# Cross attention on one core: the vector engine's out-projection work moved behind the low halves of K and of the weights

## The chip, the cores and the metric

One core of a Trainium2 chip runs the whole program in one launch. The metric is the device time in microseconds; the median of three runs stands for a kernel. The engines run side by side and meet through semaphores: TensorE (PE, with its weight loads as PEld), VectorE (DVE), ScalarE (ACT), GpSimd (POOL) and the queue engine SyncE (SP).

## The reference

Three layers with residuals follow each other; the change sits in the first, a cross attention of 16 batches: 64 latent rows (x) each look at 512 context rows plus the latents themselves, 8 heads of 64, everything in fp32.

```
x = x + xattn(ctx, layernorm(x), mask)
x = x + attn(layernorm(x))
x = x + ffn(layernorm(x))        # weights and activations in blockwise FP4

# xattn
xn = LN(ctx) * g_x + b_x ;  ln = LN(latents) * g_l + b_l
q = ln @ w_q ;  k, v = split(concat(xn, ln) @ w_kv)
attn = softmax(q k^T * scale, masked)
out = LN((attn v) @ w_out) * g_o + b_o

# fp4_quant_dequant of a weight, in blocks of 16
scale = max|w| / 6 ;  wn = w / scale ;  q = nearest E2M1 value(wn) * scale
```

## The kernel before

An fp32 product is computed as three matmuls on a high part (rounded to fp32r) and a low part (what the rounding left): high by high, high by low, low by high. `mm3` (L142) issues them; in the profile they are the lines L146, L147 and L148. ACT copies a result out of PSUM and so rounds it to its high half. DVE subtracts the high half from the full value and gets the low half: `split_lo` (L786, its instruction at L788). A transpose on PE is L412.

The order of the work on every engine is written out by hand as one software pipeline. A loop over batches b = 0 to 16 contains eight slots each. In slots 0 to 3 PE projects the keys of batch b, 128 rows at a time (`project_k`), after weighing the values of batch b-1. In slots 4 to 7 it computes the scores, transposes the next batch's normalised context and projects values. The FP4 quantisation of the FFN weights is woven in: 34 jobs of 11 DVE steps, a transpose on PE and a split into `sb_w_hi` (ACT) and `sb_w_lo` (DVE), laid out by `weight_plan` (L101), at most four steps a slot.

PE writes into PSUM banks 4 to 7, taken in turn (`Ring`, L87). A bank that is to be written for the second time waits until the unit that used it has been drained, and a key tile is drained only by DVE's low half of K (`lo_of_k`, L809).

Batches are finished in pairs: two of them make one tile of 128 rows. For a tile, the out-projection's work is spread over two loop turns. In an even turn b: `out_split` (L849, slot 5), the matmul (slot 6), and `out_stats` (L854, slot 7). In the odd turn behind it: `out_scale` (L860, slot 0) normalises `sb_y_row` (L762) and multiplies it by g_o (L864). POOL adds b_o (`shift_y`, L1603, instruction L1605). `out_add` (L866, slot 1) adds the residual (L869) and takes the statistics of the sum (L749, L755, L757).

POOL's own order in slot 0 of an odd turn is: store the weight job's halves to DRAM (`spill_weight`, L1607, two DMAs that wait for `sb_w_lo`), then the addition of b_o, and, in slot 1, the power that turns the next batch's variances into reciprocal roots (`sb_b_rstd`, L1578), which waits for DVE's `sb_b_ve` (L757).

In the same slots DVE also normalises the context of batch b+1 (`normalise`, L813): two statistics in slot 0, two in slot 1 with the four L755 and the L757 of `finish_stats`, and the four normalisations (L762 on `sb_ctx`) in slots 2 and 3. PE's transposes in slot 4 need all four.

Of the kernel before, what the change touches and what calls it, by code (L numbers as in the profile page):

```python
# [44 lines left out]
TURN_STEP, SPLIT_STEP = QUANT_STEPS, QUANT_STEPS + 1  # L45
# [55 lines left out]
def weight_plan():  # L101

    plan, at = {}, [0, 0]

    def advance(key, count):
        plan[key] = []
        for _ in range(count):
            if at[0] == NJ:
                return
            job, step = at  # L110
            plan[key].append((job, step))
            at[:] = [job + 1, 0] if step == SPLIT_STEP else [job, step + 1]
            if step + 1 == TURN_STEP:
                plan[key].append((job, TURN_STEP))
                at[1] = SPLIT_STEP
                return

    for b in range(1, NB):
        for slot in range(8):
            if slot != 3 or b % 2:  # L120
                advance((b, slot), 4)
    assert at[0] == NJ
    return plan


WEIGHTS = weight_plan()
# [40 lines left out]
def perceiver(nc, a, out):  # L167
    ctx = ExitStack()
    with ctx:
# [569 lines left out]
        def vector_program(e):  # L739
# [8 lines left out]
            def small_stats(src, i, st):  # L748
                e.bn_stats(st[0][:, i, :], src).then_inc(dve_chain.up())  # L749

            def finish_stats(first, n, st):
                stats, mv, ve, rstd = st
                for i in range(first, first + n):
                    on.wait_ge(dve_chain.sem, dve_chain.value)
                    e.bn_aggr(mv[:, i, :], stats[:, i, :]).then_inc(dve_chain.up())  # L755
                on.wait_ge(dve_chain.sem, dve_chain.value)
                e.tensor_scalar(ve[:, first:first + n], mv[:, first:first + n, 1], EPS_LN, None, ALU.add).then_inc(rstds.up())  # L757
                return rstds.value
# [27 lines left out]
            def split_lo(full, hi, lo, hi_sem, hi_value, done):  # L786
                on.wait_ge(hi_sem, hi_value)
                e.tensor_tensor(lo, full, hi.bitcast(F32), ALU.subtract).then_inc(done)  # L788
# [20 lines left out]
            def lo_of_k(b, n):  # L809
                bank, nth = took["k", b, n]  # L810
                split_lo(psum[:, bank, :], k_hi[:, n, context_keys], k_lo[:, n, context_keys], k_hi_done, C * b + n + 1, drained[bank])

            def normalise(b):  # L813
                src = [ctx_in[b % 2][:, k, :] for k in range(CS)]
                on.wait_ge(ctx_landed[b % 2], 16 * (b // 2 + 1))
                on.wait_ge(z_normed, CS * b)
                for i in range(CS):
                    small_stats(src[i], i, small_b)
                    yield
                nth = finish_stats(0, CS, small_b)  # L820
                yield
                for i in range(CS):
                    normal(src[i], src[i], i, small_b, nth, z_normed)
                    yield
# [17 lines left out]
            def normalise_p(b, n):  # L842
                i, j, idx = b % 2, n % 2, C * b + n
                on.wait_ge(exped, idx + 1)
                e.reciprocal(row_inv[:, n:n + 1], row_sum[i][:, n:n + 1]).then_inc(row_inverted)
                on.wait_ge(row_inverted, idx + 1)
                e.tensor_scalar(probs[j][:, :], probs[j][:, :], row_inv[:, n:n + 1], None, ALU.mult).then_inc(p_normed)

            def out_split(t):  # L849
                on.wait_ge(tile_hi_done, t + 1)  # L850
                attn = x3[:, t, :].rearrange("p (c n) -> p c n", c=C)
                e.tensor_tensor(tile_lo[:, :, :], attn, tile_hi[:, :, :].bitcast(F32), ALU.subtract).then_inc(tile_lo_done)

            def out_stats(t):  # L854
                bank, nth = took["y", t]
                on.wait_ge(drained[bank], nth)
                small_stats(y_row[:, :], t, small_o)
                return finish_stats(t, 1, small_o)
# [77 lines left out]
            def lo_of_weight(job):  # L936
                width = JOBS[job][4]
                bank, nth = took["w", job]
                k = width // P
                ps = psum[:, bank, 0:width].rearrange("p (m n) -> p m n", n=P)  # L940
                split_lo(ps, w_hi[:, 0:k, :], w_lo[:, 0:k, :], wt_hi_done, job + 1, drained[bank])
# [156 lines left out]
            def lam_products():  # L1098
                on.wait_ge(row_consts_landed, 128)
                for k in range(2):  # L1100
                    e.tensor_tensor_reduce(lams[:, 2 * k, :], lams[:, 2 * k, :], lams[:, 2 * k + 1, :], 1.0, 0.0, ALU.mult, ALU.add,
                                           lam[:, k:k + 1]).then_inc(lam_dots)

            def lam_difference():
                on.wait_ge(lam_exped, 1)
                e.tensor_tensor(lam[:, 4:5], lam[:, 2:3], lam[:, 3:4], ALU.subtract).then_inc(dve_chain.up())
                on.wait_ge(dve_chain.sem, dve_chain.value)
                e.tensor_scalar(lam[:, 5:6], lam[:, 4:5], LAMBDA_INIT, None, ALU.add).then_inc(lam_ready)
                e.tensor_scalar(lnwb[:, :], lnwb[:, :], 1.0 - LAMBDA_INIT, None, ALU.mult).then_inc(lnw_ready)

            def zero_pack(i):
                for h, r in enumerate(HEAD_ROWS):
                    e.memset(q_pack[i][r, :, :, HEAD_ROWS[1 - h]].bitcast(U32), 0).then_inc(q_zeroed[i])
                e.memset(vl_pack[i][LQ:P, :], 0.0).then_inc(b_zeroed)
# [35 lines left out]
            for b in range(NB + 1):  # L1150
                cur, old, nxt = b < NB, b >= 1, b + 1 < NB
                t_new = (b - 2) // 2 if b % 2 == 0 and b >= 2 else None
                t_out = (b - 3) // 2 if b % 2 == 1 and b >= 3 else None
                norm = normalise(b + 1) if nxt else iter(())
                for slot in range(8):
                    if old and slot == 0:
                        normalise_p(b - 1, 3)
                    if cur and slot >= 5:
                        normalise_p(b, slot - 5)
                    if b == 0 and slot == 3:  # L1160
                        lam_products()
                        for i in range(QK_BUFFERS):
                            on.wait_ge(qk_spilled[i], 32 if i < C else 16)
                        on.wait_ge(last_keys_spilled, 16 * C)
                        for h in range(2):
                            on.wait_ge(vl_spilled[h], 64)
                        zero_pack(1)
                        for i in range(2):
                            e.memset(p_t[i][LQ:P, CS, :], 0.0).then_inc(p_zeroed)
                    if b == 2 and slot == 2:  # L1170
                        lam_difference()
                    if cur and slot == 2:
                        mask_row(b)
                    if cur and slot >= 4:
                        largest(b, slot - 4)
                    if nxt and slot >= 4:
                        lo_of_z(b + 1, slot - 4)
                    advance(norm, (2, 3, 2, 9)[slot] if slot < 4 else 0)
                    for job, step in WEIGHTS.get((b, slot), ()):
                        if step < QUANT_STEPS:  # L1180
                            next(weight_steps)
                    if t_new is not None:
                        if slot == 5:
                            out_split(t_new)
                        if slot == 7:
                            o_nth = out_stats(t_new)
                    if t_out is not None:
                        if slot == 0:
                            out_scale(t_out, o_nth)
                        if slot == 1:  # L1190
                            out_add(t_out)
                    if cur and slot < 4:
                        lo_of_k(b, slot)
                    for job, step in WEIGHTS.get((b, slot), ()):
                        if step == SPLIT_STEP:
                            lo_of_weight(job)
                    if not cur:
                        if slot == 0:
                            normal_y(0)
                        advance(steps, 1)  # L1200
# [669 lines left out]
```

## Time and profile before

| what | us |
|---|---|
| median of 3 runs (lowest, highest) | 1054.09 (1053.99, 1055.0) |
| the profiled execution's own time | 1053.52 |
| its span, from the first to the last instruction | 1051.7 |
| PE busy | 998.7 |
| DVE busy | 781.1 |
| ACT busy | 434.1 |
| POOL busy | 146.3 |

PE is busy for 95% of the span, DVE for 74%. The granted clock of PE was at its upper level but for short stretches, 0.990 in the mean. The loop over batches that the change touches takes the time from about 90 to 690 us of the span. Times in rows are microseconds from the start of the span. In a row of the timeline the first number is the start, the second the duration; consecutive instructions of one engine overlap a little in it, because an instruction's record begins while its predecessor drains. The chain of waits has the same instructions without that overlap, and "issue" in it is time for which the profile shows no reason.

### The profile page before, as it was taken

What the parts mean: (1) busy time and instruction counts of PE and PEld (TensorE: products, weight loads), DVE (VectorE), ACT (ScalarE), POOL (GpSimd) and SP (SyncE); (2) the same over time, 40 slices, a digit from 0 to 9 for tenths busy, and PEclk for the clock granted to TensorE, in tenths of its full rate; (3) what the DMA queues carried; (4) which work ended last, traced back from release to release, by engine and by line L of the source; (5) the groups of instructions that cost most, each with busy time, mean ns of one, the idle gap of its engine ahead of it and who ended that gap; (6) DMA issues with size and microseconds to landing.
All of it is one profiled execution on the core that took longest, in us unless ns stands there. A gap on an engine that the chain in (4) does not pass through costs nothing.

```text
span 1051.7 us, 16613 instructions
## 1 busy us (share of the span) xinstructions
PE 998.7 (95%) x6468; PEld 783.2 (74%) x6468; DVE 781.1 (74%) x1672; ACT 434.1 (41%) x811; POOL 146.3 (14%) x163
## 2 busy tenths in 40 slices
PE   5999999999999999999999999999999879999997
PEld 4887888788788787887887888645555558888885
DVE  6455687896987987987988864276477578998984
ACT  3534565466446445644653653222232222222211
POOL 1310011210210211202111110032132000000000
PEclk9999999999999999999999999999999889999999
DMA  7856242342442444244434323070000350000000
GB/s 242 242 160 195 75 128 65 108 126 63 128 129 74 105 118 120 65 120 121 108 83 106 111 81 110 20 271 1 2 2 16 145 206 25 10 11 11 11 11 20
DMA packets 72446, 98.50 MB, mean 94 GB/s; under 512 B 38320, under 2 KB 47152, under 8 KB 70064
## 3 DMA queue, kind: packets, MB, share of 16 engines
q1 hardware_dynamic: 65008, 72.80, 23.5%
q0 software_dynamic: 7360, 24.65, 7.4%
q8 instruction: 51, 0.84, 0.3%
q14 instruction: 27, 0.22, 0.1%
HBM read 67.54 MB, written 29.88 MB: 93 GB/s over the span
## 4 chain that ended last, share of the span: by engine, by line
PE 73%; DVE 17%; ACT 5%; issue 3%; DMA 1%; SPq 0%; POOL 0%; DVEq 0%; ACTq 0%
PE ps_banks L146 15%; PE ps_banks L148 15%; PE ps_banks L147 15%; PE ps_banks L531 10%; PE ps_banks L412 7%; PE ps_banks L508 2%; PE ps_banks L654 2%; PE ps_banks L653 2%; PE ps_banks L655 2%; DVE sb_b_stats L749 1%; PE ps_banks L429 1%; DVE sb_wq_big L915 1%; DVE sb_w_q L923 1%; DVE sb_ctx L762 1%; DVE sb_kT_lo L788 1%
## 5 line engine op out<-in xcount | busy, mean ns | idle before, releaser
L146 PE MATMUL ps_banks<-sb_zT_hi,sb_wkv_hi 128*128 128x512 f32 x256 | 105.9, 414 | 6.1 <-DVE sb_kT_lo L788 6.1
L146 PE MATMUL ps_banks<-sb_wkv_hi,sb_zT_hi 128*128 128x512 f32 x256 | 104.8, 409 | 0.0
L148 PE MATMUL ps_banks<-sb_wkv_hi,sb_zT_lo 128*128 128x512 f32 x256 | 100.4, 392 | 0.0
L148 PE MATMUL ps_banks<-sb_zT_hi,sb_wkv_lo 128*128 128x512 f32 x256 | 100.2, 391 | 0.0
L147 PE MATMUL ps_banks<-sb_zT_lo,sb_wkv_hi 128*128 128x512 f32 x256 | 100.0, 391 | 0.0
L147 PE MATMUL ps_banks<-sb_wkv_lo,sb_zT_hi 128*128 128x512 f32 x256 | 99.8, 390 | 0.0
L1252 ACT ACTIVATE sb_kT_hi<-ps_banks 128x512 fp32r<-128x512 f32 x64 | 38.1, 596 | 145.4 <-PE ps_banks L148 145.4
L146 PE MATMUL ps_banks<-sb_wgu,sb_z_hi 128*128 128x512 f32 (+1 forms) x192 | 74.3, 387 | 1.0 <-DVE sb_z_lo L788 1.0
L147 PE MATMUL ps_banks<-sb_wgu,sb_z_hi 128*128 128x512 f32 (+1 forms) x192 | 72.6, 378 | 0.0
L148 PE MATMUL ps_banks<-sb_wgu,sb_z_lo 128*128 128x512 f32 (+1 forms) x192 | 72.6, 378 | 0.0
L839 DVE CUSTOM_DVE_ANT_0 sb_probs<-ps_banks,sb_maskbias 128x576 f32<-128x576 f32 x64 | 48.1, 751 | 29.3 <-PE ps_banks L148 29.3
L788 DVE TENSOR_TENSOR sb_zT_lo<-sb_zfull,sb_zT_hi 128x512 fp32r<-128x512 f32 x64 | 44.2, 691 | 31.4 <-ACT sb_zT_hi L1296 31.4
L788 DVE TENSOR_TENSOR sb_kT_lo<-ps_banks,sb_kT_hi 128x512 fp32r<-128x512 f32 x64 | 43.7, 683 | 31.4 <-ACT sb_kT_hi L1252 30.9
L1292 ACT ACTIVATE sb_zfull<-ps_banks,sb_cols 128x512 f32<-128x512 f32 x64 | 49.8, 778 | 29.5 <-PE ps_banks L412 29.5
L146 PEld LDWEIGHTS ps_banks<-sb_zT_hi,sb_wkv_hi 128*128 128x128 f32 x256 | 48.1, 188 | 17.9 <-DVE sb_kT_lo L788 7.7
L1252 ACT ACTIVATE sb_probsT<-ps_banks 128x512 f32<-128x512 f32 (+1 forms) x128 | 47.8, 430 | 27.3 <-PE ps_banks L412 27.3
L148 PEld LDWEIGHTS ps_banks<-sb_wkv_hi,sb_zT_lo 128*128 128x128 f32 x256 | 48.0, 188 | 10.8
L148 PEld LDWEIGHTS ps_banks<-sb_zT_hi,sb_wkv_lo 128*128 128x128 f32 x256 | 48.0, 188 | 10.6
L1316 ACT ACTIVATE sb_probs<-sb_probs,sb_neg_max 128x576 f32<-128x576 f32 x64 | 49.7, 776 | 12.9 <-DVE sb_neg_max L839 12.3
L147 PEld LDWEIGHTS ps_banks<-sb_wkv_lo,sb_zT_hi 128*128 128x128 f32 x256 | 48.3, 189 | 8.4
L147 PEld LDWEIGHTS ps_banks<-sb_zT_lo,sb_wkv_hi 128*128 128x128 f32 x256 | 48.2, 188 | 8.2
L146 PEld LDWEIGHTS ps_banks<-sb_wkv_hi,sb_zT_hi 128*128 128x128 f32 x256 | 48.2, 188 | 8.1
(228 smaller groups left out, 2425.0 us busy)
## 6 DMA issues: line engine op xcount, KB each, us to landing
sb_ctx<-in_ctx SPq DMA_DIRECT2D x16, 1024.0 KB, 5.9
sb_wgu<-scratch_wgu SPq DMA_DIRECT2D x8, 1024.0 KB, 9.1
scratch_wgu<-sb_w_hi POOLq DMA_DIRECT2D x22, 256.0 KB, 3.2
scratch_wgu<-sb_w_lo POOLq DMA_DIRECT2D x22, 256.0 KB, 3.2
sb_wdn<-scratch_wdn SPq DMA_DIRECT2D x2, 2816.0 KB, 13.1
scratch_q<-sb_a_qk POOLq DMA_DIRECT2D x8, 512.0 KB, 6.2
sb_qpack<-scratch_q SPq DMA_DIRECT2D x32, 128.0 KB, 5.9
sb_wgu<-scratch_wgu SPq DMA_DIRECT2D x4, 768.0 KB, 13.8
```

The source lines that it names most:

```text
L146: e.matmul(o, wh, xh, start=i == 0, stop=False)
L147: e.matmul(o, wh, xl, start=False, stop=False)
L148: m = e.matmul(o, wl, xh, start=False, stop=i == n - 1)
L412: m = e.transpose(psum[:, bank, k * P:(k + 1) * P], s, ident[:, :])
L508: m = e.matmul(o_space(r, n), value, p_t[j][:, k, r], start=k == CS, stop=k == CS - 1)
L531: m = e.matmul(o, w[:, c, :], x[:, c, :], start=c == 0, stop=c == C - 1)
L653: e.matmul(psum[:, bank, :], h_hi[:, c, :], wdn[0][:, c, :], start=first, stop=False)
L788: e.tensor_tensor(lo, full, hi.bitcast(F32), ALU.subtract).then_inc(done)
L839: e.tensor_tensor_reduce(blocks(probs[j][:, :], WIDE // 2), s_space[j], blocks(mask_bias[:, keys(b)], WIDE // 2), -1.0, F32_MAX, ALU.add, ...
L1252: e.activation(dst, src, ACT.Identity).then_inc(done)
L1292: e.activation(z_full[j][:, :], psum[:, bank, :], ACT.Identity, bias=cols[:, 1, c:c + 1], scale=cols[:, 0, c:c + 1]).then_inc(act_chain.up())
L1316: e.activation(probs[j][:, :], probs[j][:, :], ACT.Exp, bias=neg_max[:, n:n + 1], scale=-1.0, accum_out=row_sum[b % 2][:, n:n + 1]).then_i ...
```

## The change

Inside a slot of DVE's loop, three calls trade places with two others. `out_scale`, `out_add` and `out_stats` now stand behind `lo_of_k` and `lo_of_weight`; `out_split` stays in front. Nothing is added or removed, and no other engine's program differs.

```
                     for job, step in WEIGHTS.get((b, slot), ()):
                         if step < QUANT_STEPS:
                             next(weight_steps)
-                    if t_new is not None:
-                        if slot == 5:
-                            out_split(t_new)
-                        if slot == 7:
-                            o_nth = out_stats(t_new)
+                    if t_new is not None and slot == 5:
+                        out_split(t_new)
+                    if cur and slot < 4:
+                        lo_of_k(b, slot)
+                    for job, step in WEIGHTS.get((b, slot), ()):
+                        if step == SPLIT_STEP:
+                            lo_of_weight(job)
+                    if t_new is not None and slot == 7:
+                        o_nth = out_stats(t_new)
                     if t_out is not None:
                         if slot == 0:
                             out_scale(t_out, o_nth)
                         if slot == 1:
                             out_add(t_out)
-                    if cur and slot < 4:
-                        lo_of_k(b, slot)
-                    for job, step in WEIGHTS.get((b, slot), ()):
-                        if step == SPLIT_STEP:
-                            lo_of_weight(job)
```

The first place is DVE in slot 0 of an odd turn (b = 3, 5, ..., 13; at 15 there is no weight). `sb_kT_lo` and `sb_w_lo` are the low halves of K and of the weight, `sb_y_row` the out-projection's row, `sb_b_stats` the next context's statistics.

```order
 L887 TENSOR_SCALAR sb_wq_scale<-sb_wq_amax 128x32
 L891 RECIPROCAL sb_wq_inv<-sb_wq_scale 128x32
+L788 TENSOR_TENSOR sb_kT_lo<-ps_banks,sb_kT_hi 128x512
+L788 TENSOR_TENSOR sb_w_lo<-ps_banks,sb_w_hi 128x512
 L762 TENSOR_SCALAR sb_y_row<-sb_y_row,sb_lo_mv,sb_lo_rstd 128x512
 L864 TENSOR_TENSOR sb_y_row<-sb_y_row,sb_g_o 128x512
-L788 TENSOR_TENSOR sb_kT_lo<-ps_banks,sb_kT_hi 128x512
-L788 TENSOR_TENSOR sb_w_lo<-ps_banks,sb_w_hi 128x512
 L749 BN_STATS sb_b_stats<-sb_ctx 128x6 x2
 L755 BN_AGGR sb_b_mv<-sb_b_stats 128x2 x4
```

Both low halves move ahead of the two instructions on `sb_y_row`; what stands before and behind the four is as it was.

The second place is DVE in slot 1 of the same turns. `sb_x` is the residual tile, `sb_ly_...` its statistics.

```order
 L904 TENSOR_SCALAR sb_wq_big<-sb_wq_mag 128x512
 L907 TENSOR_SCALAR sb_wq_mag<-sb_wq_mag 128x512
+L788 TENSOR_TENSOR sb_kT_lo<-ps_banks,sb_kT_hi 128x512
 L869 TENSOR_TENSOR sb_x<-sb_x,sb_y_row 128x512
 L749 BN_STATS sb_ly_stats<-sb_x 128x6
 L755 BN_AGGR sb_ly_mv<-sb_ly_stats 128x2
 L757 TENSOR_SCALAR sb_ly_ve<-sb_ly_mv 128x1
-L788 TENSOR_TENSOR sb_kT_lo<-ps_banks,sb_kT_hi 128x512
 L830 TENSOR_SCALAR sb_maskbias<-sb_mask 128x512
```

The low half of the second key tile moves ahead of the four instructions of `out_add`. In slot 7 of the even turns nothing changes places, since neither a key tile nor a weight's split falls into it.

## Rows read from the trace of the kernel before

**Rows 1.** The page: busy time of each engine, share of the span, instructions
```profile
PE 998.7 (95%) x6468; PEld 783.2 (74%) x6468; DVE 781.1 (74%) x1672; ACT 434.1 (41%) x811; POOL 146.3 (14%) x163
```

**Rows 2.** Who PE waited for, whole span: total us, times, longest
```profile
PE ps_banks L146 <- DVE sb_kT_lo L788: 6.1, 6, 1.1
...
PE ps_banks L412 <- DVE sb_w_q L923: 3.5, 5, 0.8
```

**Rows 3.** Timeline of PE in turn 3: start, us, [idle before <- releaser]
```profile
193.79 0.27 PE L494 MATMUL ps_banks<-sb_ident,sb_probs 128*64 128x128 f32 x1
195.16 0.50 PE L146 MATMUL ps_banks<-sb_zT_hi,sb_wkv_hi 128*128 128x512 f32 x1 [1.09 <-DVE sb_kT_lo L788]
...
206.22 0.66 PE L412 MATMUL ps_banks<-sb_ident,sb_w_q 128*128 128x128 f32 x4 [0.69 <-DVE sb_w_q L923]
```

**Rows 4.** The chain that ended last, turn 3: start, us, what
```profile
193.41 0.38 DVE sb_y_row L762
...
193.81 0.69 DVE sb_y_row L864
194.50 0.60 DVE sb_kT_lo L788
195.10 0.60 DVE sb_w_lo L788
...
197.79 1.02 DVE sb_b_ve L757
198.81 0.60 DVE sb_wq_xn L895
...
206.76 0.92 DVE sb_ctx L762 x2
```

**Rows 5.** Timeline of ACT in turn 3
```profile
192.24 0.60 ACT L1252 ACTIVATE sb_kT_hi<-ps_banks 128x512 fp32r<-128x512 f32 x1 [1.58 <-PE ps_banks L148]
192.73 0.59 ACT L1252 ACTIVATE sb_w_hi<-ps_banks 128x512 fp32r<-128x512 f32 x1
```

**Rows 6.** Timeline of POOL in turns 3 and 5
```profile
195.99 0.73 POOL L131 DMA_DIRECT2D scratch_wgu<-sb_w_hi  x1 [4.93 <-DVE sb_w_lo L788]
196.67 0.80 POOL L131 DMA_DIRECT2D scratch_wgu<-sb_w_lo  x1
197.32 1.45 POOL L1605 TENSOR_TENSOR sb_y_row<-sb_y_row,sb_b_o 128x512 f32<-128x512 f32 x1
198.89 1.54 POOL L1578 TENSOR_TENSOR sb_b_rstd<-sb_b_ve,sb_half_pow 128x4 f32<-128x4 f32 x1
...
271.72 1.45 POOL L1605 TENSOR_TENSOR sb_y_row<-sb_y_row,sb_b_o 128x512 f32<-128x512 f32 x1
```

**Rows 7.** Busy time of `sb_b_ve` by stretch, first and last of the six odd turns, and their sum
```profile
197.70:198.90 1.20, 1.02 (x1) 1.00 0.85 256
...
568.50:569.70 1.20, 1.08 (x1) 1.00 0.89 282
sum 7.30, DVE 6.40; mean DVE 1.07
```

**Rows 8.** Timeline: `sb_b_ve` in the even turn 4 with POOL behind it, and in turn 5
```profile
232.54 0.17 DVE L757 TENSOR_SCALAR sb_b_ve<-sb_b_mv 128x4 f32<-128x4 f32 x1
232.79 1.03 POOL L1578 TENSOR_TENSOR sb_b_rstd<-sb_b_ve,sb_half_pow 128x4 f32<-128x4 f32 x1 [9.53 <-DVE sb_b_ve L757]
...
272.07 1.13 DVE L757 TENSOR_SCALAR sb_b_ve<-sb_b_mv 128x4 f32<-128x4 f32 x1
```

**Rows 9.** Timeline of DVE in turns 2, 3 and 4; all but 202.98 beside POOL's DMAs
```profile
161.53 1.44 DVE L762 TENSOR_SCALAR sb_ctx<-sb_ctx,sb_b_mv,sb_b_rstd 128x512 f32<-128x512 f32 x2
...
202.98 1.00 DVE L762 TENSOR_SCALAR sb_ctx<-sb_ctx,sb_b_mv,sb_b_rstd 128x512 f32<-128x512 f32 x2
...
211.20 0.68 DVE L895 SCALAR_TENSOR_TENSOR sb_wq_xn<-sb_w_in,sb_wq_inv 128x512 f32<-128x512 f32 x1
...
235.47 1.05 DVE L762 TENSOR_SCALAR sb_ctx<-sb_ctx,sb_b_mv,sb_b_rstd 128x512 f32<-128x512 f32 x2
```

## The prediction

> **What bounds the kernel now.** I read the page first: PE is busy for 95% of the span and DVE for 74% [rows 1], so a change in DVE's order can pay only where PE waits for DVE, or where DVE itself gets shorter in a stretch that PE then waits for. The list of PE's waits comes next [rows 2]: six waits of at most 1.1 us for `sb_kT_lo`, 6.1 us in all, and 3.5 us for the quantised weight `sb_w_q`. Both belong to the odd turns.
>
> PE's timeline of turn 3 shows how the two are placed [rows 3]. PE has done its transposes at 194.06 (193.79 + 0.27), is stopped until 195.16 because the bank of the second key projection is drained only by `sb_kT_lo`, works without a gap, and is stopped again for 0.69 until 206.22, now for `sb_w_q`.
>
> The chain of waits for the same stretch says what sets the end [rows 4]. It never leaves DVE from 193.41 (and before) until the last normalised context rows at 207.68 (206.76 + 0.92), which PE needs for its next transposes. So slots 0 to 3 of an odd turn are bound by the sum of DVE's instructions, not by PE's matmuls. One of them is strange: `sb_b_ve`, 128 x 4 numbers, takes 1.02 us. In the even turn 4 it takes 0.17 [rows 8]. Over the six odd turns it takes 6.40 us [rows 7]. The timeline of POOL gives the reason that I take [rows 6]: from 197.32 POOL adds b_o to the 128 x 512 row, until 198.77 (197.32 + 1.45), and `sb_b_ve` ends at 198.81, 0.04 later. In turn 5 the addition ends at 273.17 (271.72 + 1.45) and `sb_b_ve` at 273.20 (272.07 + 1.13). The DVE instruction is held while POOL's addition runs; in even turns there is no addition and no hold.
>
> **The change part by part.** It adds and removes no instruction; all its terms are waits.
>
> Slot 0, the two low halves earlier. They move ahead of two instructions that take 194.50 - 193.41 = 1.09 us [rows 4]. Their own inputs are there: ACT has K's high half at 192.84 and the weight's at 193.32 [rows 5], and DVE would come to them at 193.41 and 194.01. So `sb_kT_lo` would be finished at 194.01 instead of 195.10, PE could go on at about 194.1, and the 1.09 us of PE's stop is gone, 6.1 us over six turns.
>
> What is late next is `sb_w_q`. It is DVE's, and for DVE nothing has become shorter by the exchange alone. PE would come to it 1.05 us earlier and wait 0.69 + 1.05 = 1.74 us for it. By this step alone the change is worth 0: the 6.1 us come back at the weight's transpose.
>
> Slot 0, what POOL does. POOL's two DMAs wait for `sb_w_lo`. That ended at 195.70 and the first DMA began at 195.99; now it ends at 194.61 and they begin at 194.90. The addition of b_o stands behind them in POOL's order and also waits for the product with g_o, which now ends where `sb_w_lo` ended, at 195.70. The DMAs kept POOL until 197.47 (196.67 + 0.80), now until 196.38, so they and not the product still decide: the addition moves by the whole 1.09 us and ends at 197.68 instead of 198.77.
>
> `sb_b_ve` is reached by DVE at 197.79 as before, since the same instructions stand ahead of it. It no longer meets the addition. In turn 5, the tightest I found, the addition would end at 272.08 and `sb_b_ve` begins at 272.07, a hold of 0.01. The hold is therefore gone in all six turns: 6.40 us less six times 0.17 = 5.38 us of DVE's chain [rows 7, 8].
>
> Does PE follow? Its new slack before `sb_w_q` is 1.74 us, more than the 0.85 to 0.96 us that DVE gains in a turn, so `sb_w_q` and the context rows stay the last things to come and PE moves up with them by the whole amount. After slot 3 the loop runs on PE again and the lead is kept.
>
> What can take some of it back is the new neighbourhood of POOL's DMAs. They used to run beside statistics; now they begin at 194.90 beside the end of the normalisation of `sb_y_row` (194.61 to 194.99), and the product with g_o. Nearest rows: a pair of such normalisations takes 1.00 us alone, 1.05 beside DMAs in turn 4, and 1.44 in turn 2 [rows 9]. An instruction with two inputs from SBUF, `sb_wq_xn`, took its normal 0.68 beside a DMA. The cost for six turns lies between 0 and 6 x 0.44 = 2.6 us. I take the nearer row, turn 4, where DVE's instruction began before the DMA as it will here: 6 x 0.05 = 0.3 us.
>
> Here a rule of the Trainium skill speaks against the change. Its page "SBUF — State Buffer", section "Who interferes with whom", says that a VectorE instruction in a two-port mode and GpSimd lock each other out of a shared port pair, whoever starts first, and that descriptors of a DMA issued by GpSimd cannot be written meanwhile. By it the DMAs would start writing only at 194.99 (0.09 later), the addition would end at 197.77, and up to 0.1 us of hold would stay in turns such as the fifth: an estimate of 0.6 us less gain. The 1.44 of turn 2 agrees that the two can meet; the unchanged 0.68 beside a DMA fits its remark that two-input instructions only share a read side.
>
> Slot 1. `sb_kT_lo` of the second tile moves ahead of the four instructions of `out_add`. DVE does not wait there before or after; PE's third and fourth projections did not wait for it [rows 2, 3]. Its ACT half is ready, because PE's second projection starts 1.05 us earlier. The addition of b_o, which `out_add` needs, ends even earlier. 0 us. Turn 15 has neither a weight nor a next context, and PE has no such wait there: 0 us. The last tile's calls stand outside the loop: 0 us.
>
> The sum. The profiled execution took 1053.5 us for a span of 1051.7. 1053.5 - 5.4 + 0.3 = 1048.4. The median of the runs lies 0.6 above that execution (1054.1), so for a median I say **1049.0 us**.
>
> **The rivals.** A: the hold moves instead of going. Right behind `sb_b_ve` stands `sb_wq_xn` with two inputs from SBUF, and POOL's power for `sb_b_rstd` starts 0.08 us after `sb_b_ve` ends; alone it takes 1.03 us [rows 8], in turn 3 it took 1.54 [rows 6], since DVE was there first. If POOL gets in first, or if the hold has a cause other than the addition, DVE's chain keeps its length, and with the first step's 0 the time is about 1054.1; at the worst, held for 1.1 us each, 6 x 1.1 - 5.4 = 1.2 more, 1055.3. Against it: the order of the two starts depends only on the end of `sb_b_ve`, as before. Chance 13%.
>
> B, the slower side: the two DMAs of POOL hold the product with g_o until both are written, 196.38 instead of a start at 195.01. That is 1.37 us of DVE's chain in a turn, 6 x 1.37 = 8.2, against 5.4 gained: 2.8 us slower, 1056.9. It loses as soon as the hold is longer than 0.90 us a turn. For it: 1.44 in turn 2. Against it: the 0.68 and the 1.05 [rows 9]. Chance 5%.
>
> C: in between, the DMAs cost 0.44 in every turn: 1054.1 - 5.4 + 2.6 = 1051.3. Chance 9%.
>
> D: only PE's 6.1 us of waits count and DVE's chain isn't the bound, as a reader of the list of waits alone would say: 1054.1 - 6.1 = 1048.0. The chain speaks against it, the time would hardly tell it from mine; the wait for `sb_w_q` would. Chance 3%.
>
> **How the numbers follow.** My forecast has 70%, with a range of its own from 1047.8 (no cost, runs 0.9 lower) to 1050.3. To leave out no more than 2 in 10 the range needs C and stops below A: 1047.5 to 1053.2. What lies outside is A and B, 18%. A measurement here tells 0.2% (2.1 us) from no change. Faster are my forecast, C and D: 82%, of which 1 goes to no change, since C may stay smaller than it can be told; the same is A with it, 14%; slower is B, 5%.
>
> **What would show it.** `sb_b_ve` at 0.17 in odd turns and six starts of the addition about 1.1 us earlier against it: the second step. No wait of PE for `sb_kT_lo`, and waits for `sb_w_q` of about 0.9 instead of 0.7 us: the first. Normalisation and product of `sb_y_row` at 0.38 and 0.69 in the chain: the cost. I am wrong if `sb_b_ve` or `sb_wq_xn` still takes about 1 us, if the product takes over 1 us, or if PE comes to `sb_w_q` after it is ready.

## The result and the profile after

The changed kernel takes 1047.6 us (median of 6 runs, 1043.21 to 1048.52) against 1054.13 us (6 runs): a ratio of 0.9946, interval 0.9922 to 0.9970, so 3 to 8 us faster. The ratio on record is not the plain quotient of these two medians, which is 0.9938. In a later set of runs it came to 0.9948 (0.9929 to 0.9967). Single executions of one kernel lie 5 to 6 us apart here and up to 7.5 us in the later sets, and their mean granted clock goes from 0.990 to 0.998. I therefore read the size of each effect from a stretch of the loop in each trace, beside the timed ratio.

The profiled execution took 1048.52 us, its span is 1046.7 us. PE's waits for `sb_kT_lo` [rows 2] are no longer in the list; those for `sb_w_q` grew from 3.5 to 5.4 us. Columns as in [rows 2]:

```profile
PE ps_banks L412 <- DVE sb_w_q L923: 5.4, 6, 1.0
```

PE's timeline of turn 3 answers to [rows 3]. The second key projection follows the transposes at once, and the next stop is 1.03 us long:

```profile
194.99 0.27 PE L494 MATMUL ps_banks<-sb_ident,sb_probs 128*64 128x128 f32 x1
195.20 0.50 PE L146 MATMUL ps_banks<-sb_zT_hi,sb_wkv_hi 128*128 128x512 f32 x1
...
206.61 0.66 PE L412 MATMUL ps_banks<-sb_ident,sb_w_q 128*128 128x128 f32 x4 [1.03 <-DVE sb_w_q L923]
```

The chain of waits still runs through DVE in this stretch, as in [rows 4], but `sb_b_ve` is short:

```profile
194.60 0.55 DVE sb_kT_lo L788
195.15 0.59 DVE sb_w_lo L788
195.74 0.47 DVE sb_y_row L762
...
196.23 0.69 DVE sb_y_row L864
...
199.02 0.17 DVE sb_b_ve L757
199.19 0.60 DVE sb_wq_xn L895
...
207.16 0.92 DVE sb_ctx L762 x2
```

The instructions of `sb_b_ve` as a group (duration least, median, greatest in ns; [rows 7] had six of over 1000):

```profile
L757 DVE TENSOR_SCALAR sb_b_ve<-sb_b_mv x16: 170/170/171, 62.4 to 599.0; 128x4 f32<-128x4 f32 x16
```

POOL's timeline of turn 3 [rows 6]: the addition ends at 197.37 + 1.45 = 198.82, and `sb_b_ve` starts 0.20 us later. In the kernel before it started 0.47 us behind the start of the addition (197.79 against 197.32), now 1.65 us behind it.

```profile
196.04 0.73 POOL L131 DMA_DIRECT2D scratch_wgu<-sb_w_hi  x1 [3.78 <-DVE sb_w_lo L788]
196.71 0.80 POOL L131 DMA_DIRECT2D scratch_wgu<-sb_w_lo  x1
197.37 1.45 POOL L1604 TENSOR_TENSOR sb_y_row<-sb_y_row,sb_b_o 128x512 f32<-128x512 f32 x1
199.27 1.54 POOL L1577 TENSOR_TENSOR sb_b_rstd<-sb_b_ve,sb_half_pow 128x4 f32<-128x4 f32 x1 [0.44 <-DVE sb_b_ve L757]
```

**Where the 5 us are.** From PE's first transpose of a weight in turn 3 to the first matmul of the last tile's out-projection, the kernel before took 680.46 - 192.04 = 488.42 us, the changed one 676.75 - 193.23 = 483.52 us. The rows of the changed kernel:

```profile
193.23 0.60 PE L412 MATMUL ps_banks<-sb_ident,sb_w_q 128*128 128x128 f32 x4
...
676.75 0.50 PE L146 MATMUL ps_banks<-sb_w_out_hi,sb_tile_hi 128*128 128x512 f32 x1 [1.54 <-DVE sb_tile_lo L852]
```

So the loop gives 4.90 us. Outside it the head was 1.19 us longer and the tail 1.29 us shorter (1051.7 - 680.46 against 1046.7 - 676.75); the two execute the same program there. The clock explains part of the tail, which has one stretch of 3.4 us at the lower level less. It doesn't explain the head: there the kernel before has such a stretch, at 16.8 us, the changed one has none, and yet it is the longer. These two differences cancel by luck; the change does not act there.

### The profile page after: what moved, and what is told of

It reads as the page before. It is cut to its first block, busy times and chain, and to the rows that moved or that the text cites. A ratio compares the mean times of both kernels' runs of the same rounds, so it can differ in the third digit from the quotient of the medians.

```text
span 1046.7 us, 16613 instructions
## 1 busy us (share of the span) xinstructions
PE 997.9 (95%) x6468; PEld 783.4 (75%) x6468; DVE 776.0 (74%) x1672; ACT 434.1 (41%) x811; POOL 147.8 (14%) x163
## 4 chain that ended last, share of the span: by engine, by line
PE 74%; DVE 17%; ACT 5%; issue 3%; DMA 1%; SPq 0%; POOL 0%; DVEq 0%; ACTq 0%
PE ps_banks L146 15%; PE ps_banks L148 15%; PE ps_banks L147 15%; PE ps_banks L531 10%; PE ps_banks L412 7%; PE ps_banks L508 2%; PE ps_banks L654 2%; PE ps_banks L653 2%; PE ps_banks L655 2%; DVE sb_b_stats L749 1%; PE ps_banks L429 1%; DVE sb_wq_big L915 1%; DVE sb_w_q L923 1%; DVE sb_ctx L762 1%; DVE sb_kT_lo L788 1%
```

## The experiments

Each run was timed beside the kernel before on the same chip, in 6 to 12 executions. The first four share one chip, the last four another. "Loop" is the stretch just defined, from each kernel's own profile.

| kernel | ratio to before (interval) | loop, us | PE's waits for kT_lo / w_q, us | sum of `sb_b_ve`, six odd turns, us |
|---|---|---|---|---|
| before | 1 | 488.42 | 6.1 / 3.5 | 6.40 |
| changed | 0.9946 (0.9922 to 0.9970) | 483.52 | 0 / 5.4 | 1.02 |
| slot 0 only | 0.9938 (0.9914 to 0.9961) | 483.51 | 0 / 5.3 | 1.02 |
| slot 1 only | 0.9997 (0.9976 to 1.0017) | 488.66 | 6.1 / 3.6 | 6.40 |
| K's half only | 1.0023 (1.0006 to 1.0040) | 492.85 | 0 / 10.7 | 6.43 |
| POOL adds first | 0.9939 (0.9915 to 0.9964) | 483.31 | 6.1 / 0 | 1.02 |
| hold put back | 0.9970 (0.9954 to 0.9986) | 486.45 | 0 / 8.3 | 3.95 |
| out_add in even turns | 0.9869 (0.9837 to 0.9900) | 475.10 | 0 / 0 | 1.02 |
| same, old order | 0.9943 (0.9924 to 0.9962) | 481.92 | 6.1 / 0 | 1.02 |
| changed, again | 0.9948 (0.9929 to 0.9967) | 483.49 | 0 / 5.3 | 1.02 |

**One slot at a time.** DVE's loop, the exchange in slot 0 only:

```
+                    if t_out is not None and slot == 1:
+                        out_add(t_out)
                     if cur and slot < 4:
                         lo_of_k(b, slot)
...
                             lo_of_weight(job)
+                    if t_out is not None and slot == 0:
+                        out_scale(t_out, o_nth)
```

> Only the exchange in slot 0 (both low halves ahead of the out-projection's scaling); in slot 1 the order is as before the change. Hold theory (POOL's addition of b_o holds sb_b_ve; moving sb_w_lo forward moves POOL's DMAs and with them the addition out of its way): sb_b_ve at 0.17 us in all six odd turns, no wait of PE for sb_kT_lo, and the whole gain, about 1048.5 us. Rival, that slot 1 has a share (its four instructions no longer ahead of the second low half of K): 1050 to 1052, with new waits of PE in slots 2 or 3.

And in slot 1 only (the two calls the other way round):

> Only the exchange in slot 1; in slot 0 the order is as before the change. Hold theory: sb_b_ve stays at about 1.06 us in six turns, PE waits 6.1 us in all for sb_kT_lo, the time is that of the kernel before, 1054 us. Rival, that slot 1 has a share: 1050 to 1052.

Slot 0 has the whole gain (loop 483.51 against 483.52), slot 1 none (488.66 against 488.42, with the waits of before). So slot 1 has no share.

**PE's waits without the hold's end.** Only K's low half goes ahead of the scaling:

```
                     if cur and slot < 4:
                         lo_of_k(b, slot)
+                    if t_out is not None and slot == 0:
+                        out_scale(t_out, o_nth)
                     for job, step in WEIGHTS.get((b, slot), ()):
                         if step == SPLIT_STEP:
                             lo_of_weight(job)
```

> In slot 0 only the low half of K moves ahead of the scaling; the weight's low half stays behind it; slot 1 as before the change. Hold theory: PE's six waits for sb_kT_lo (6.1 us) are gone, but POOL's DMAs and the addition start as before, sb_b_ve keeps 1.02 to 1.13 us, and the wait for sb_w_q grows from 0.7 to 1.8 us a turn: 1054 us, no gain. Rival, that the waits of PE are what pays: 1048 us, waits for sb_w_q unchanged.

This parts the two things that the change does at once. All of PE's waits for `sb_kT_lo` are gone and nothing is gained; the time is even 0.2% longer. Its chain in turn 3 keeps the long `sb_b_ve`:

```profile
193.36 0.46 DVE sb_y_row L762
...
193.84 0.69 DVE sb_y_row L864
194.54 0.60 DVE sb_w_lo L788
...
197.23 1.02 DVE sb_b_ve L757
```

The 6.1 us came back at the transpose of the weight: its waits grew by 7.2 us, from 3.5 to 10.7. Columns as in [rows 2], then PE's timeline of turns 3 and 5:

```profile
PE ps_banks L412 <- DVE sb_w_q L923: 10.7, 6, 2.0
```

```profile
205.66 0.66 PE L412 MATMUL ps_banks<-sb_ident,sb_w_q 128*128 128x128 f32 x4 [1.88 <-DVE sb_w_q L923]
...
281.73 0.66 PE L412 MATMUL ps_banks<-sb_ident,sb_w_q 128*128 128x128 f32 x4 [1.99 <-DVE sb_w_q L923]
```

In this execution the loss above zero is the clock. From 1.8 us behind the stop of turn 3 the granted clock of PE is at its lower level of 1.2 GHz; in the stretches below (from:to, length, busy time of PE, PEld, DVE, ACT, POOL, each with its count, then PEclk) it is 0.50 from 208 to 210:

```profile
204.00:206.00 2.00, 0.34 (x3) 0.34 (x4) 1.86 (x4) 1.10 (x2) 0.00 (x0) 1.00 0.00 0
206.00:208.00 2.00, 1.94 (x14) 1.70 (x13) 1.93 (x6) 0.89 (x3) 0.00 (x0) 0.85 0.56 146
208.00:210.00 2.00, 2.00 (x6) 1.55 (x6) 2.00 (x4) 1.45 (x2) 0.24 (x1) 0.50 0.07 18
```

That happened in turns 3, 5 and 7 of this execution, 3.4 us each. What they cost is read from the distance between the transposes of the weight in two turns:

```profile
432.97 0.66 PE L412 MATMUL ps_banks<-sb_ident,sb_w_q 128*128 128x128 f32 x4 [1.87 <-DVE sb_w_q L923]
...
506.79 0.66 PE L412 MATMUL ps_banks<-sb_ident,sb_w_q 128*128 128x128 f32 x4 [1.78 <-DVE sb_w_q L923]
```

The kernel before has these transposes at 429.18 and 502.94. From turn 3 to turn 9, with three low stretches between, this run takes 432.97 - 205.66 = 227.31 us and the kernel before 429.18 - 206.22 = 222.96: 4.35 longer. From turn 9 to turn 11, without one, it is 73.82 against 73.76. The loop as a whole is 4.4 us longer, so without the low stretches K's half alone is worth about 0. None of the other traces has a low stretch inside the loop.

**The hold's end without PE's waits.** DVE as before the change; in POOL's program one call moves:

```
+                    if t_out is not None and slot == 0:
+                        shift_y(t_out)
                     for job, step in WEIGHTS.get((b, slot), ()):
                         if step == SPLIT_STEP:
                             spill_weight(job)
```

> The order of DVE as before the change; in POOL's slot 0 the addition of b_o stands ahead of the two DMAs of the weight. Hold theory: the addition runs about 194.8 to 196.1 in turn 3, sb_b_ve drops to 0.17 us in six turns, DVE's chain is 0.85 to 0.96 us a turn shorter. PE keeps its six waits for sb_kT_lo (6.1 us) and so comes to sb_w_q when it is ready: of the gain PE can use 0.65 to 0.7 us a turn, about 4 us: 1050 us. Rival, that only PE's waits for sb_kT_lo pay: 1054 us.

The direction held, and the size was larger than expected: 5.1 us of the loop instead of 4, as much as the whole change. PE still loses 6.1 us to `sb_kT_lo`, and every wait for `sb_w_q` has vanished. POOL's timeline and the chain in turn 3:

```profile
193.89 1.28 POOL L1605 TENSOR_TENSOR sb_y_row<-sb_y_row,sb_b_o 128x512 f32<-128x512 f32 x1 [3.52 <-DVE sb_y_row L864]
195.31 0.73 POOL L131 DMA_DIRECT2D scratch_wgu<-sb_w_hi  x1
```

```profile
197.11 0.17 DVE sb_b_ve L757
...
205.22 0.92 DVE sb_ctx L762 x2
206.15 0.04 issue
206.19 0.66 PE ps_banks L412 x4
```

My 4 us took the 0.69 us of wait from the timeline for all the room that PE had. The record of the last matmul before it, 205.14 to 205.53 in the kernel before, ends with its modelled tail; in the chain one matmul follows another after 0.23 us, so PE could have gone on at 205.37, 0.16 us sooner. That makes 0.85 us in turn 3, which is what the hold's end gives there.

**The hold put back.** The changed kernel, with one more instruction in POOL's slot 0, whose result nobody reads:

```
                         if slot == 0:
+                            e.tensor_tensor(pad[:, :], b_o[:, 0:PAD], b_o[:, 0:PAD], ALU.add)
                             shift_y(t_out)
```

> The changed kernel with one more POOL instruction (an addition of 128 x 384 numbers into a tile that nobody reads) between the weight's DMAs and the addition of b_o, which so runs a good 1 us later, where it ran before the change. DVE's order is the changed one. Hold theory: sb_b_ve is held again, for 0.9 to 1.2 us in six turns, PE has no wait for sb_kT_lo and waits 1.8 to 2.0 us a turn for sb_w_q, the gain is gone: 1053 to 1056 us. The upper end if PE's clock falls to its lower level after waits of that length, as in the run with K's half alone moved. Rival, that DVE's own order gives the gain: 1048 us.

It delays the addition by 0.79 us (it starts 2.12 us after the first DMA instead of 1.33), less than I had counted on, so the hold came back only in part and the time with it. The busy time of `sb_b_ve` by stretch, as in [rows 7]:

```profile
190.00:202.00 12.00, 0.61 (x1) 1.00 0.62 173
...
sum 99.00, DVE 3.95; mean DVE 0.66
```

I had expected the whole gain to go; a little over half of the hold came back. What did come back is paid in full: the hold is 3.95 - 1.02 = 2.93 us, and the loop is 486.45 - 483.52 = 2.93 us longer than the changed kernel's. In turn 3 the addition ends at 195.02 + 1.45 = 196.47 and `sb_b_ve` at 195.89 + 0.61 = 196.50:

```profile
195.02 1.45 POOL L1606 TENSOR_TENSOR sb_y_row<-sb_y_row,sb_b_o 128x512 f32<-128x512 f32 x1
```

```profile
195.89 0.61 DVE L759 TENSOR_SCALAR sb_b_ve<-sb_b_mv 128x4 f32<-128x4 f32 x1
```

DVE's order is the changed one here, and the loop follows the hold, so the order as such did not give the gain. Nor is the hold a wait that the program asks for: `finish_stats` (L751) lets `sb_b_ve` wait for DVE's own statistics alone, for nothing of POOL's.

**DVE's chain made shorter.** If DVE bounds these slots, work taken out of them must pay until PE has no stop left. `out_add` goes to slot 3 of the next even turn (with it POOL's power for `sb_ly_rstd`), ahead of K's low half, where DVE idled 2.08 us:

```
+                t_add = (b - 4) // 2 if b % 2 == 0 and b >= 4 else None
...
+                    if t_add is not None and slot == 3:
+                        out_add(t_add)
                     if cur and slot < 4:
                         lo_of_k(b, slot)
...
-                        if slot == 1:
-                            out_add(t_out)
```

> The changed kernel with out_add taken out of the odd turns and put into slot 3 of the next even turn, ahead of the low half of K, where DVE waited 2.1 us for ACT. Theory that DVE's chain bounds slots 0 to 3 of the odd turns: it is 1.6 us a turn shorter, more than PE's remaining wait for sb_w_q (1.03 us), so that wait is gone, and 1.0 us a turn is gained over the changed kernel: about 6 us, 1042 us at the same clock. sb_kT_lo in slot 3 of the even turns is not later. Rival, that the time moves to the even turns: 1048 us, with a new wait of PE there.

This is the fastest kernel of the study, 1035.68 us (median of 6) and 0.9869 of the kernel before on the same chip, where the changed kernel had 0.9948. Its loop is 8.4 us shorter than the changed kernel's, more than the 6 I expected. PE's starts in the two traces, compared one by one, show where: in turn 3 PE gains 1.19 us at the transposes of the weight, not 1.03, for the reason given above, and another 0.28 at the transposes of the context, which had waited for DVE's last rows without a stop that the list shows. The four instructions of `out_add` take 1.62 us of the changed kernel's chain (201.37 to 202.99), 9.7 over six turns; not all of it pays, because the chain has now gone over to PE. In turn 3 it holds PE's matmuls alone from 196 to 206:

```profile
200.48 0.43 PE ps_banks L146
...
203.43 0.44 PE ps_banks L412 x4
```

In the even turn the added work fits before K's high half is there; DVE's remaining idle time in front of `sb_kT_lo` is 0.35 us:

```profile
236.35 0.68 DVE L869 TENSOR_TENSOR sb_x<-sb_x,sb_y_row 128x512 f32<-128x512 f32 x1
...
238.02 0.15 DVE L757 TENSOR_SCALAR sb_ly_ve<-sb_ly_mv 128x1 f32<-128x1 f32 x1
238.52 0.69 DVE L788 TENSOR_TENSOR sb_kT_lo<-ps_banks,sb_kT_hi 128x512 fp32r<-128x512 f32 x1 [0.35 <-ACT sb_kT_hi L1251]
```

The same with the old order of DVE's slot 0 and POOL's addition first:

> As the run before, with out_add in the even turns, but DVE's order of slot 0 as before the change (scaling ahead of the low halves) and POOL's addition ahead of its DMAs, so that the hold is gone as well. Now DVE's chain is short and PE's waits for sb_kT_lo (1.0 us in six turns) should be what bounds: about 6 us slower than the run before, 1048 us. Rival, that these waits are free here too: 1042 us.

Both have `sb_b_ve` at 0.17 and no wait for `sb_w_q`. Here the waits for `sb_kT_lo` do cost: 481.92 - 475.10 = 6.8 us of the loop for 6.1 us of waits.

```profile
PE ps_banks L146 <- DVE sb_kT_lo L788: 6.1, 6, 1.1
```

So the exchange of the low halves, as a cure for PE's wait, is worth nothing in the kernel it was made for and about 7 us once DVE's chain has been shortened.

**The changed kernel again**, beside these:

> The changed kernel itself, unaltered, on the chip of these runs: 0.5% under the kernel before, sb_b_ve at 0.17 us in the odd turns.

It repeats its loop to 0.03 us and its ratio to 0.0002.

## Why the prediction was right

**What bounds the stretch.** Right: DVE's chain in slots 0 to 3 of the odd turns. K's half alone gave nothing, a hold of 2.93 us cost 2.93 us, and `out_add` taken out of the chain paid until PE had no stop left.

**The exchange by itself worth 0.** Right. PE's stop for `sb_kT_lo` disappeared and its stop for `sb_w_q` grew. It grew to 1.03 us in turn 3, where I had said about 0.9 after the hold's end; without that end it was 1.88, where I had said 1.74.

**The hold of `sb_b_ve`.** Right in place, cause and size. All six fell to 0.17 us, 5.38 us of DVE's time. The cause was tested from both sides: moving only POOL's addition takes the hold away, delaying only the addition brings it back to the extent of the overlap.

**What takes some of it back.** I had put 0.3 us for POOL's DMAs in their new neighbourhood. The normalisation of `sb_y_row` takes 0.47 us in the chain instead of 0.38 [rows 4], 0.54 us over six turns, and 4.90 of the 5.38 are left. The size was near and the reason wrong. With K's half alone moved it takes 0.46, and there the DMAs begin 1.6 us after its end. In turn 15 of the changed kernel, where no DMA of POOL's is near, its record is as long as in turn 3:

```profile
633.39 0.54 DVE L762 TENSOR_SCALAR sb_y_row<-sb_y_row,sb_lo_mv,sb_lo_rstd 128x512 f32<-128x512 f32 x1
```

That is the usual length of such an instruction. The 64 normalisations of the context, of the same shape, take (least, median, greatest in ns):

```profile
L762 DVE TENSOR_SCALAR sb_ctx<-sb_ctx,sb_b_mv,sb_b_rstd x64: 537/543/823, 63.7 to 605.6; 128x512 f32<-128x512 f32 x64
```

So the exception is the kernel before. There it stood right behind the RECIPROCAL on 128 x 32 numbers (L891), and its record is 0.45 us long, 0.38 in the chain. My sum took this short form along to a place where it does not occur; 0.92 for two such instructions in [rows 4], 0.46 each, would have told me. Why it is shorter behind the reciprocal stays open.

The product with g_o kept its 0.69, so rival B, that POOL's DMAs hold it, did not occur. Nor did the delay that the Trainium skill let me expect ("SBUF — State Buffer", "Who interferes with whom": a VectorE instruction in a two-port mode starves GpSimd of the port time in which it generates descriptors). The addition starts 1.33 us after the first DMA in both kernels, 197.32 - 195.99 and 197.37 - 196.04. It is a weak test, since the normalisation (195.66 to 196.20) overlaps the first DMA by 0.16 us only. The exclusive lock on a shared port pair that the same section of the Trainium skill describes, by which the later of the two is blocked until the first is done, is what the hold of `sb_b_ve` looks like; the runs show the hold, not the port.

**Rival A**, that the hold moves to `sb_wq_xn`, did not occur: it takes 0.60 us in the chain as before. **Rival D**, that PE's 6.1 us pay, is refuted by K's half alone, though 1048.0 us would have been the nearest of all numbers to the 1047.6 measured. A time alone would have confirmed it.

**The sum.** 1049.0 against 1047.6. The loop accounts for 4.90 us of the 5.1 in the sum. The profiled execution took 1048.52, where the sum has 1048.4; that they are so near is in part luck, since the head's 1.19 us and the tail's 1.29, which have nothing to do with the change, cancel. The 0.6 that I added for the median had the wrong sign: this time the median lies 0.9 below the profiled execution. The difference between the two medians, 6.5 us, is larger than the effect in the loop and within the interval of 3 to 8.

## What to carry to other kernels

When an instruction takes several times what its like takes elsewhere, look at what POOL does in that time before counting its duration as work: here 0.85 to 0.96 us in each of six turns, hidden in a busy time. And when an instruction moves, take its duration from its like in the new place, not from its own in the old one. A wait that an engine has for another is worth removing only if the other's chain is not what it meets next; test it by removing the wait alone. A reorder also has effects on engines whose programs it does not touch, through the semaphores they start from.

## What the runs showed of the hardware that I had not expected

A VectorE instruction on 128 x 4 numbers took up to 1.13 us instead of 0.17 beside a GpSimd addition. In the changed kernel the statistics (L749, 1.21 us for two in the chain) and their aggregation (L755, 0.19 us each) ran beside the same addition at their usual durations.

Stops of PE of 1.88, 1.99 and 1.88 us (turns 3, 5 and 7) were followed by 3.4 us at the lower clock. In the same execution one of 1.87 us (turn 9) was not, nor was one of 1.78 (turn 11): the length of the stop alone doesn't tell. Stops of up to 1.6 us, with the hold put back, were not followed by one in the execution profiled.

A normalisation of 128 x 512 fp32 numbers, 0.46 to 0.47 us in the chain elsewhere, took 0.38 us right behind a reciprocal of 128 x 32 numbers.
